# The first attention of a four-layer kernel: sums of the exponentials over two halves, the second norm and a unit's last steps a tick later

## The reference

```python
# x: (16, 256, 128), after a layer norm; a second norm follows here
mu = jnp.mean(x, axis=-1, keepdims=True)
var = jnp.mean(jnp.square(x - mu), axis=-1, keepdims=True)
xn = (x - mu) * jax.lax.rsqrt(var + LN_EPS) * gamma
q = (xn @ w_q).reshape(b, n, HEADS, DIM_HEAD).transpose(0, 2, 1, 3)   # 16 heads of 64
...                                                # k, v; two null keys and values per head
q = _l2norm(q) * q_scale
k = _l2norm(k) * k_scale
sim = jnp.einsum('bhid,bhjd->bhij', q, k) * ATTN_SCALE
...                                                # distance slopes, causal mask
attn = jax.nn.softmax(sim, axis=-1)
out = jnp.einsum('bhij,bhjd->bhid', attn, v)
out = out.transpose(0, 2, 1, 3).reshape(b, n, HEADS * DIM_HEAD)
return out @ w_out
```

## Time and profile before

| | |
|---|---|
| median of 3 runs | 2493.4 us (2490.78 to 2494.09) |
| profiled execution | 2489.9 us, of it a span of 2488.3 us |
| TensorE busy | 93% of the span |
| first attention | its steady part runs from about 90 to 700 us, 46.7 us per sequence |
| granted TensorE clock there | 1.00 |

### The profile page before, as it was taken

How to read it: one execution, slowest core, us unless ns; L and a number is a source line. 1 busy time by engine, 2 the same in 40 slices (tenths; PEclk the granted TensorE clock), 3 DMA queues, 4 the chain that set the end, 5 groups by cost and what they waited for, 6 DMA issues and landing times. The chain is left out here.

```text
span 2488.3 us, 60369 instructions
## 1 busy us (share of the span) xinstructions
PE 2321.6 (93%) x23146; PEld 1789.9 (72%) x23209; DVE 1620.9 (65%) x4106; ACT 1480.6 (60%) x2973; POOL 1588.5 (64%) x2537
## 2 busy tenths in 40 slices
PE   6999999999998999988999999999999968699997
PEld 5778878878876556656777787777778757566665
DVE  5666666666674578874454577777777732478786
ACT  5666666666664478874444466666666523377775
POOL 6788888888885364443333277777777732366664
PEclk9999999999999989999999999999999989899999
DMA  8950000000000010001000000000000036100000
GB/s 284 331 170 2 2 2 2 2 2 2 2 2 1 1 47 2 2 2 33 1 1 1 3 4 4 6 6 4 6 6 4 6 99 182 58 11 10 8 4 35
DMA packets 22911, 83.84 MB, mean 34 GB/s; under 512 B 3969, under 2 KB 10754, under 8 KB 21474
## 3 DMA queue, kind: packets, MB, share of 16 engines
q1 hardware_dynamic: 19474, 72.76, 9.0%
q0 software_dynamic: 3152, 7.21, 0.9%
HBM read 72.75 MB, written 46.79 MB: 48 GB/s over the span
## 5 line engine op out<-in xcount | busy, mean ns | idle before, releaser
L982 POOL TENSOR_TENSOR XR<-XR,T 128x256 f32<-128x256 f32 x504 | 368.4, 731 | 37.7 <-DVE T L861 8.0
L725 ACT ACTIVATE P<-ps 128x384 f32<-128x384 f32 (+1 forms) x512 | 250.5, 542 | 194.8 <-PE ps L2761 191.5
L2761 PE MATMUL ps<-P,V 128*64 128x256 f32 (+3 forms) x4096 | 334.3, 348 | 0.8 <-ACT P L725 0.7
L1529 DVE TENSOR_REDUCE bm<-ps 128x3 f32<-128x384 f32 x512 | 260.3, 550 | 52.4 <-PE ps L2761 49.7
L2761 PEld LDWEIGHTS ps<-P,V 128*64 128x64 f32 (+1 forms) x4096 | 185.9, 123 | 123.1 <-issue 46.3
L1469 ACT ACTIVATE P<-ps 128x768 f32<-128x768 f32 x256 | 207.5, 811 | 76.3 <-PE ps L2761 71.0
L892 DVE TENSOR_REDUCE sm<-ps 128x2 f32<-128x512 f32 (+1 forms) x256 | 129.8, 548 | 168.5 <-PE ps L2761 168.5
L1636 POOL TENSOR_SCALAR_AFFINE_SELECT P<-P 128x512 f32<-128x512 f32 x256 | 165.4, 647 | 103.1 <-ACT P L1469 101.5
L995 POOL TENSOR_TENSOR PS<-P 128x256 f32<-128x256 f32 x256 | 181.3, 732 | 69.1 <-ACT P L725 68.8
L1016 POOL TENSOR_TENSOR ss<-ss,nhalf 128x16 f32<-128x16 f32 x64 | 187.7, 2932 | 5.3
L2761 PE MATMUL ps<-mk,identb 128*128 128x256 bf16 (+1 forms) x768 | 174.8, 296 | 15.2 <-DVE bm L1529 9.0
(11 more groups left out here) (315 smaller groups left out, 6792.8 us busy)
## 6 DMA issues: line engine op xcount, KB each, us to landing
rows_i<-in_zero SPq DMA_DIRECT2D x16, 1208.0 KB, 30.9
rows_o<-in_zero SPq DMA_DIRECT2D x16, 1208.0 KB, 80.5
w<-in_m_w SPq DMA_DIRECT2D x23, 578.0 KB, 4.0
zt<-rows_i SPq DMA_DIRECT2D x23, 128.0 KB, 3.1
rows_o<-yo POOLq DMA_DIRECT2D x23, 128.0 KB, 3.8
stg<-in_t_w SPq DMA_DIRECT2D x11, 256.0 KB, 2.8
XR<-in_x SPq DMA_DIRECT2D x4, 512.0 KB, 9.2
out<-XR SPq DMA_DIRECT2D x8, 256.0 KB, 2.0
```

Of the source, the lines that this page charges most:

```text
L725: e.activation(self.P[at % 6][:, :], K.ps.ap("st", s, g, h)[:, 0:self.w], ACT.Exp, bias=0.0, scale=1.0 if kind == 0 else 0.125).then_inc(K ...
L982: p = po.e.tensor_tensor(x, x, self.T[g % 2][:, par, pr], ALU.add)
L1529: e.tensor_reduce(bm[:, h, :], K.ps.ap("mx", s, g, h)[:, 0:384].rearrange("p (a c) -> p a c", c=128), X, ALU.max, negate=True).then_inc(K. ...
L2761: return self.te.matmul(o, l, r, start=start, stop=True, skip_group_check=True)
```

## The change

The unit's step `sm` becomes its own, at tick 21; `sT` moves to tick 22 and `out` to 23, and a unit has 25 ticks in place of 24. DVE gets four additions per unit, one for each head, of P's columns 128 to 255 and 256 to 383 into a new tile PS, in the ticks after the two `st` ticks. The sums then take eight matmuls of 128 columns (four on P, four on PS) in place of four of 256 and four of 128. The second norm's z moves from tick 4 to 5 and its transpose (`zT_at`) from 6 to 7. Three one-time pieces of set-up work are placed to match (`mid_dve`, the first sequence's norm, the early list).

```diff
-            first, last, unit = 8, 13, 24
-            self.tk = {"qk": 0, "turn": 6, "mx": 9, "v": 12, "mT": 15, "st": 17, "pv": 20, "sT": 21, "out": 22}
+            first, last, unit = 8, 13, 25
+            self.tk = {"qk": 0, "turn": 6, "mx": 9, "v": 12, "mT": 15, "st": 17, "pv": 20, "sm": 21, "sT": 22, "out": 23}
...
-        self.zT_at, self.sn_at = (6, 12) if kind == 0 else (4, 99)
+        self.z2_at, self.zT_at, self.sn_at = (5, 7, 12) if kind == 0 else (99, 4, 99)
...
+            self.PS = [sb(f"PS{s}_{i}", [128, 4, 128], F32) for i in range(2)]
+            self.halved = K.sem(f"halved{s}")
...
-        if kind == 0:
-            for kt, q, c, w in self.blocks():
-                for h in range(4):
-                    p = K.acc(sm[32 * h:32 * h + 32, q:q + w], self.one[:, 0:32], P[h][:, c:c + w], start=kt == 0)
-            p.then_inc(K.ps.full_of("sm", s, g), 1)
...
         pe.wait_ge(self.halved, 4 * g + 4)
         for h in range(4):
-            p = K.acc(sm[32 * h:32 * h + 32, 0:256], self.one[:, 0:32], self.PS[g % 2][:, h, :], start=True)
+            r = slice(32 * h, 32 * h + 32)
+            if self.kind == 0:
+                K.acc(sm[r, 0:128], self.one[:, 0:32], self.P[(4 * g + h) % 6][:, 0:128], start=True)
+            else:
+                p = K.acc(sm[r, 0:256], self.one[:, 0:32], self.PS[g % 2][:, h, :], start=True)
+        for h in range(4 if self.kind == 0 else 0):
+            p = K.acc(sm[32 * h:32 * h + 32, 128:256], self.one[:, 0:32], self.PS[g % 2][:, h, :])
...
-        if self.kind == 0 and k == 4:
+        if k == self.z2_at:
...
+        n = self.part("st", k - 1)
+        if kind == 0 and n is not None:
+            if g >= 2:
+                dv.wait_ge(*K.ps.filled("sm", s, g - 2))
+            for h in (2 * n, 2 * n + 1):
+                P = self.P[(4 * g + h) % 6]
+                dv.wait_ge(*K.ps.read("st", s, g, h))
+                e.tensor_tensor(self.PS[g % 2][:, h, :], P[:, 128:256], P[:, 256:384], ALU.add).then_inc(self.halved, 1)
```

More of the change, by code:

```diff
@@ L272, in is_early @@
         if self.kind == 0:
-            return name == "prep" and a[0] == 0 and k in (0, 2, 4)
+            return name == "prep" and a[0] == 0 and k in (0, 2, self.z2_at)
         return self.kind == 2 and name == "prep" and a[0] < 2 and k in (0, 2, 4)
@@ L547, in pe_pv @@
         pv = K.ps.take(pe, self.G, "pv", s, g)
-        sm = K.ps.take(pe, self.G, "sm", s, g) if kind == 0 else None
         pe.wait_ge(self.one_in, 1)
@@ L729, in act_unit @@
                 ac.wait_ge(*K.ps.filled("Y", s, g - 2, 1))
-                if kind == 0:
-                    ac.wait_ge(*K.ps.filled("sT", s, g - 2))
             ac.wait_ge(*K.ps.filled("pv", s, g))
@@ L734, in act_unit @@
                          ACT.Copy).then_inc(K.ps.out_of("pv", s, g), 1)
-        if self.part("pv" if kind == 0 else "sm", k) is not None:
-            if kind == 2 and g >= 2:
+        if self.part("sm", k) is not None:
+            if g >= 2:
                 ac.wait_ge(*K.ps.filled("sT", s, g - 2))
@@ L770, in dve_prep @@
             e.tensor_copy(self.bias[:, :], K.ps.ap("bias")[:, 0:128]).then_inc(K.ps.out_of("bias"), 1)
-        if self.kind == 0 and b == 0 and k == 7:
-            K.mid_dve(dv)
         if self.kind == 0 and b == 0 and k == 12:
@@ L800, in dve_prep @@
             i.then_inc(K.ps.out_of("zT", s, b), 1)
+            if self.kind == 0 and b == 0:
+                K.mid_dve(dv)
     def dve_unit(self, dv, b, u, k):
@@ L933, in pool @@
                 n = K.nb[s] + (4 if self.kind == 0 else 2) * a[0]
-                if self.kind == 0 and k in (1, 3) and not self.is_early(name, a, k - 1):
+                if self.kind == 0 and k in (1, 3) and a[0] > 0:
                     for i in range(2):
@@ L2857, in pre_dve @@
         self.a0_low(dv, 2).then_inc(self.a0_lo_v, 1)
-        first.dve_prep(dv, 0, 4)
+        first.dve_prep(dv, 0, first.z2_at)
         self.a0_low(dv, 3).then_inc(self.a0_lo_v, 1)
```

## The result

The changed kernel takes 2499.0 us (median of 19 runs, 2495.1 to 2513.2); the kernel before took 2492.6 in the same session. The ratio is 1.0031, 95% interval 1.0021 to 1.0041: slower by 0.3%, or 6.4 us. The prediction said 2536 with a range from 2510: right in the sign, wrong in the size and outside its range. The profiled executions differ by a little more, 2488.3 and 2498.4 us of span.

The account below looks back on a forecast made before the run. The prediction took TensorE's stream to set the pace, any wait of it costing in full. Its terms, 45.4 + 19.2 + 1.5 + 2.9 - 14.1 - 9.1 = +45.8 on 2489.9, gave 2536 us, range 2510 to 2566.

Parts of the forecast that it names:

- (a): Output projection no longer covers DVE's chain behind the rough scores; TensorE waits 0.71 us per unit at `nm`, +45.4 us.
- (b): Two additions on DVE ahead of the second maxima, held by POOL's additions, delay them 0.3 us per unit, +19.2 us.
- (c): The other two additions, between QL and KL with T behind KL; bank take hardly later, +1.5 us.
- (d): Sums behind P,V take 256 columns in place of 384, saving 0.22 us per unit, -14.1 us.
- (e): Second norm a tick later; the 0.61 us wait ahead of z's transposes goes, once per sequence, -9.1 us.
- (f): One more tick per unit, showing once, at the end, +2.9 us.
- Rival 1: At `nm`, DVE's chain needs no cover, so (a) and (b) fall: 2471 us, chance 0.07.
- Rival 2: POOL's power blocks the second pair of additions on DVE: +77 to +128, about 2636 us, chance 0.06.
- Rival 3: TensorE's clock falls for a tenth of the stage: some +35 us, about 2571 us, chance 0.06.
- Rival 4: Even: DVE is never late and half of (a) goes: +4 us, 2494 us, chance 0.08.

Follow-up runs that it names:

- e1: The kernel before with only the output projection's step (and the T multiplications and POOL additions tied to it) moved to tick 23 from 22; 2508.5 us, 1.0073.
- e2: The changed kernel with all its later ticks, but the old sums and no additions on DVE; 2488.5 us, ratio 0.9986 to the kernel before.
- e10: e2 with the change's additions kept on DVE and their result unused; 2508.9 us, ratio 1.0062 to the kernel before.
- e7: The kernel before with z at tick 5, its transposes at 7, short sums, and the second pair of additions ahead of T; 2492.6 us, 0.9994.
- e8: e7 with each addition made as a reduction of one SBUF input; 2490.9 us, ratio 0.9994 to the kernel before.
- e9: e7 with additions and short sums only in units 0 and 1 of a sequence, old sums in the others; 2476.8 us, 0.9924.
- e12: e9 with each addition made as a reduction of one SBUF input; 2472.5 us, ratio 0.9906 to the kernel before.
- e3: The kernel before with only the second norm's z at tick 5 and its transposes at 7; 2478.4 us, ratio 0.9947.
- e6: The changed kernel with additions over 8 of 128 columns, sums of queries 128 to 255 leaving out key tile 0; 2487.5 us, 0.9972 to the kernel before.

## Why the prediction was right or wrong

**(a) The projection leaves the place behind the scores, +45.4: the step that failed.** The prediction's wait of 0.71 us per unit at `nm` does not exist. "It comes there just as `nm` is ready" took two events that stood 0.03 apart in the earlier trace rows for producer and consumer. They belong to different units. The text ahead of the prediction had what was needed: `nm` is made at tick 10, transposed at tick 15, and units are 4 ticks apart. The names in the rows carry no buffer number, and the nearness of the two starts did the rest. e1, the test of just this step, measured 16 us in place of 45 and no wait at `nm` in a quiet unit. The part that is real was not in the sum: borders (below).

**(b) Additions ahead of the second maxima, +19.2.** Half right. POOL's additions do hold them, as read from the earlier trace rows: single ones up to 852 ns and 379 on average, with a median of 283. But the delay doesn't pass through `nm`. It makes the work behind it on DVE late, and this reaches TensorE only in units 2 and 3, where the norm takes the slack. The cost from the table: changed less e2 is 0.87 a sequence; the shorter sums save 0.84 (below), so the additions cost 0.87 + 0.84 = 1.71, or 26 us over fifteen. e10 gives 1.24 without the sums. That the two differ may be because a shorter stream on TensorE waits more for a late DVE; no run separates it.

**(c) T behind the additions, +1.5: mis-sized.** I set DVE's extra work against a delay of TensorE by the wait at `nm`. As this wait doesn't exist, TensorE arrives early and finds T late: 12.8 + 4.7 us of waits in 100 to 640. What the trace shows of (b) is what it shows of (c); I can't divide the 1.71 between them. Together I had 20.7 and the runs say about 26. The sum of these two terms was nearly right by luck, with the wrong path behind it.

**(d) Shorter sums, -14.1: right.** `P,one` went from 0.79 to 0.57 (0.24 for `P,one`, 0.33 for `PS,one`, start to start). The quiet units of e7, e8, e9 and e12 gained 0.21 each; four units, 0.84 a sequence, are 13 us.

**(e) The norm a tick later, -9.1: right in kind, larger.** e3 gave 13.9 us. Unit 2 gained 1.21 where I counted the 0.61 of the wait alone, and unit 3 lost 0.36. Two things were left out. "Only two places" misses a third line of the view behind the earlier trace rows, the projection's wait behind z's transposes, again once a sequence:

```profile
PE ps L2761 <- DVE sm L892: 1.7, 11, 0.2
```

And a wait costs more than the idle time beside it, since without one a block starts before the last one has ended. From start to start (medians of ten, unit 2) z's transposes came 0.99 us behind the rough scores and the projection 0.60 behind them; in e3 a block follows the rough scores after 0.22 and z's transposes after 0.22. That is about 1.15 of the 1.21. Unit 3's loss is in its first projections, 1.52 before and 1.89 in e3, where the idle time is 0.13.

**(f) One more tick, +2.9: right in size, and in part by luck.** The last `P,V` of the stage moved by 7.2 us, the last transposes of z by 4.6; the difference, 2.6, is the tail. The groups of `P,V` (first and last start), before and changed:

```profile
L2761 PE MATMUL ps<-P,V x1024: 272/326/431, 56.9 to 783.1; 128*64 128x128 f32 x86, 128*64 128x256 f32 x85
```

```profile
L2769 PE MATMUL ps<-P,V x1024: 272/326/431, 56.2 to 790.3; 128*64 128x128 f32 x86, 128*64 128x256 f32 x85
```

A tick of plain work is not what fills it. TensorE stands still for 2.22 us there, once, and behind this its granted clock is down for some 6 us (0.91, 0.50 and 0.74 in three stretches of 2 us), which costs about 1.7 us as an estimate from these rows:

```profile
726.09 0.27 PE L2772 MATMUL ps<-ident,pn 128*64 128x128 f32 x1 [2.22 <-POOL pn L1042]
```

```profile
728.00:730.00 2.00, 2.00 (x13) 1.88 (x12) 1.09 (x4) 0.87 (x2) 1.13 (x2) 0.50 0.00 0
```

The wait comes with the later ticks: all seven kernels here with `out` at 23 have it once, 1.83 to 2.75 us, and none of those with `out` at 22, which wait elsewhere in their tails (the kernel before 1.57 and 1.03 us, with the clock at 1.00). What one tick costs by itself stays open.

**The term that was missing: borders.** "Ahead of P,V, for which nothing was late" priced the projection's new place at nothing. The same matmuls in another order cost 0.24 us a unit (e2 against e3), without a wait. The starts show it where a block now follows one of another tile shape: rough scores (64*128) to the projection (64*128) 0.22, 335.97 to 336.19; rough scores to the transposes of S (128*128) 0.31 in the changed kernel's timeline, 336.09 to 336.40. The same 0.09 comes at the last of the projections of q and k (128*128), behind which `P,one` (128*32) now stands in place of `mk` (128*128), and 0.05 at the projection, behind which `P,V` now stands in place of the transposes of raw. S's transposes take 0.05 more at their new place and those of raw behind them 0.05 less. 0.24 in 64 units is 15 us. In units 2 and 3 part of it is hidden, so a sequence pays 0.44, not 0.96. That it is the tile shape is read from these places; no run changed a shape and kept the order, and what in the engine makes such a border longer was not tested.

**The ledger**, per sequence: z -0.85, the later ticks +0.44, the sums -0.84, the additions +1.71: +0.46. Fifteen sequences give 7, with the tail of 2.6 about 10. The two profiled executions differ by 10.1, but this closeness is partly chance: their last `P,V` differ by 7.2 only, and 2.9 come behind it, where apart from the last steps of a unit the change touches nothing. The additions' term closes this sum by its making. Independent of it are e10, which puts the additions at 1.24, and e6, which gets 0.80 back by shortening them, both in units 2 and 3 alone. What the ledger leaves unproven is the split of the additions' cost into DVE's own work and POOL's hold.

**The rivals.** Rival 1, `nm` needs no cover, was right in what it says of `nm`, for another reason than the one I gave it; its 2471 left out the borders and the additions. With 7 for the borders as a sequence pays them, 26 for the additions in place of the 1.5 of (c), and 12.8 in place of 9.1 for (e), it comes to 2471 + 7 + 26 - 1.5 - 3.7 = 2499; this is made up afterwards, of terms measured here. Rival 2, the power blocks the second pair, is refuted, and with it the rule that (b) quotes, as far as the power goes. All 92 additions of the second pair between 100 and 640 us lie within a power and take 257 to 286 ns; of the 92 of the first pair, beside POOL's additions, 43 take over 300. Two of them within a power:

```profile
328.38 2.94 POOL L1024 TENSOR_TENSOR ss<-ss,nhalf 128x16 f32<-128x16 f32 x1
...
328.79 0.48 DVE L834 TENSOR_TENSOR PS<-P 128x128 f32<-128x128 f32 x2
```

Rival 3, the clock: it stayed at 1.00 from 100 to 720 us and fell once in the tail, for some 1.7 us in place of 35. Rival 4's time, 2494, is nearest to the result, by a path that did not occur.

## What to carry to other kernels

Two events that stand close together in a timeline are not yet producer and consumer. With double buffers, count ticks or compare the consumer's start with the producer's end over several units, before a wait is priced. Where the load differs within a period (here the norm beside two of four units), price an addition unit by unit: the same four instructions were free in two units and cost more than they saved in the other two. Making them only where they are free took the kernel with early reductions from 0.9994 to 0.9906; z's later ticks alone, without additions, give 0.9947. The recorded idle time of a wait understated what it cost here, as it leaves out the lost overlap of neighbouring blocks: compare starts. And reordering matmuls isn't free even when nothing waits, here where blocks of unlike tile shapes became neighbours.

## What the runs showed of the hardware

- Moving blocks of matmuls so that unlike tile shapes become neighbours cost 0.24 us in a unit of 11 us with no wait, in steps of 0.09 us (64*128 to 128*128, and 128*128 to 128*32) and 0.05.
- A wait of TensorE costs more than its recorded idle time: 0.61 and 0.16 idle, and 1.15 from start to start.
- An addition of two SBUF tensors on DVE is held by POOL's additions (43 of 92 over 300 ns, up to 852) but not by POOL's power (92 within one, 257 to 286). The same addition as a reduction over one strided input is never held (393 to 426), and costs about as much.
- Cutting an addition from 128 to 8 columns took its median from 283 to 158 ns only.
